# Layernorms, first scans and head queries begun before the stage or batch ahead has ended, in an eight-stage kernel

## What is computed

```
x = x + tanh(g) * mamba0(ctx, layernorm(x))        # 16 states, scan over 512 steps; z = layernorm(x)
x = x + tanh(g) * ffn0(layernorm(x))               # silu(x Wg) * (x Wu), 2 of 4 kept, Wd
x = x + tanh(g) * attention1(layernorm(x), ctx)
x = x + tanh(g) * ffn1(layernorm(x))               # ternary weights, 1408 wide
x = x + tanh(g) * mamba2(ctx, layernorm(x))
x = x + tanh(g) * ffn8(layernorm(x))               # weights rounded to float8
x = x + tanh(g) * attention3(layernorm(x), ctx)    # 16 heads of 128, rms-normed q and k
x = x + tanh(g) * bitnet(layernorm(x))               # needs mean |w| of both weights
# mamba, for each batch and state n, over the steps t:
h[t] = h[t-1] * exp(delta[t] * A[n]) + delta[t] * u[t] * B[n, t];   y[t] += h[t] * C[n, t]
```

## Time and profile before

| | us |
|---|---|
| median of three runs | 4097.34 (4094.35 to 4101.24) |
| profiled execution | 4101.41 |
| its span | 4099.8 |
| PE busy in it | 3705.4 |

### The profile page before, as it was taken

How to read it: one execution, slowest core, us unless ns; L and a number is a source line. 1 busy time by engine, 2 the same in 40 slices (tenths; PEclk the granted TensorE clock), 3 DMA queues, 4 the chain that set the end, 5 groups by cost and what they waited for, 6 DMA issues and landing times.

```text
span 4099.8 us, 41151 instructions
## 1 busy us (share of the span) xinstructions
PE 3705.4 (90%) x12733; PEld 1930.0 (47%) x12786; DVE 2992.1 (73%) x4855; ACT 1751.3 (43%) x2729; POOL 666.2 (16%) x647
## 2 busy tenths in 40 slices
PE   5989898889999998899995899899999999999787
PEld 3565555644444444444442444455455455454343
DVE  6777777759889797889889655467377377377398
ACT  4767676742323222333441111055255255254276
POOL 1433343433324210233320000000000000000000
PEclk8999999999999999999997999999999999999899
DMA  3323222342332422443333000022012021022000
GB/s 106 111 96 110 97 103 99 127 169 88 144 148 79 156 75 69 162 176 130 142 141 149 1 1 0 27 83 73 28 55 73 19 72 55 28 72 73 0 11 31
DMA packets 92134, 346.28 MB, mean 84 GB/s; under 512 B 12161, under 2 KB 20481, under 8 KB 78497
## 3 DMA queue, kind: packets, MB, share of 16 engines
q1 hardware_dynamic: 61888, 226.90, 15.5%
q0 software_dynamic: 30048, 116.94, 8.3%
HBM read 281.40 MB, written 62.39 MB: 84 GB/s over the span
## 4 chain that ended last, share of the span: by engine, by line
PE 58%; DVE 23%; issue 10%; ACT 6%; DMA 3%; POOL 0%; DVEq 0%; ACTq 0%; SPq 0%; POOLq 0%
PE ps L1009 38%; PE ps L1354 5%; PE ps L1083 4%; PE ps L1344 3%; PE ps L1231 2%; PE ps L1179 2%; DVE room L1504 2%; DVE room L1508 2%; PE ps L1076 2%; DVE room L1512 1%; DVE stat L1466 1%; DVE room L1517 1%; DMA room<-bc_scratch 1%; ACT room L729 1%; DVE ln L1482 1%
## 5 line engine op out<-in xcount | busy, mean ns | idle before, releaser
L1009 PE MATMUL ps<-lnT,room 128*128 128x512 f32 x2240 | 989.8, 598 | 26.0 <-DVE room L1698 10.2
L1009 PE MATMUL ps<-room 128*128 128x512 bf16 (+1 forms) x2873 | 936.6, 483 | 64.9 <-DVE xres L1970 19.6
L587 POOL TENSOR_TENSOR idle<-idle 128x1 f32<-128x1 f32 x288 | 474.7, 1648 | 1501.8 <-ACT room L792 554.9
L1009 PEld LDWEIGHTS ps<-lnT,room 128*128 128x128 f32 x2240 | 426.7, 191 | 573.3 <-issue 534.0
L1009 PEld LDWEIGHTS ps<-room 128*128 128x128 bf16 (+1 forms) x2912 | 398.1, 139 | 581.8 <-issue 324.1
L1179 PE MATMUL ps<-room 128*128 128x512 f32 x864 | 378.7, 596 | 8.4 <-DVE room L1650 8.4
L666 ACT ACTIVATE room<-room,small 128x511 f32<-128x511 f32 x256 | 163.6, 709 | 365.7 <-DVE room L1508 351.4
L1009 PE MATMUL ps<-down_rows,room 128*128 128x256 f32 x1024 | 250.1, 400 | 47.6 <-ACT room L786 46.9
L1565 DVE TENSOR_TENSOR_SCAN room<-room 128x2048 f32<-128x2048 f32 x64 | 283.1, 4424 | 6.2
L1508 DVE TENSOR_TENSOR_SCAN room<-room 128x2048 f32<-128x2048 f32 x64 | 283.4, 4428 | 5.4
L1934 DVE TENSOR_REDUCE stat<-ps 128x1 f32<-128x512 f32 x256 | 177.0, 692 | 132.0 <-PE ps L1009 132.0
(11 more groups left out here) (216 smaller groups left out, 4907.3 us busy)
## 6 DMA issues: line engine op xcount, KB each, us to landing
kv_stash<-room POOLq DMA_DIRECT2D x128, 256.0 KB, 2.8
room<-in_ffn SPq DMA_DIRECT2D x16, 2048.0 KB, 10.8
room<-bc_scratch POOLq DMA_DIRECT2D x128, 256.0 KB, 3.6
room<-kv_stash SPq DMA_DIRECT2D x64, 512.0 KB, 3.5
room<-stash POOLq DMA_DIRECT2D x24, 1024.0 KB, 9.5
room<-in_ffn SPq DMA_DIRECT2D x20, 1024.0 KB, 5.0
room<-in_ffn SPq DMA_DIRECT2D x12, 1536.0 KB, 7.8
room<-bc_scratch SPq DMA_DIRECT2D x64, 256.0 KB, 3.7
```

Of the source, the lines that this page charges most:

```text
L587: nc.gpsimd.tensor_tensor(idle[:, :], idle[:, :], idle[:, :], ALU.add).then_inc(zeros_added, 1)
L1009: last = nc.tensor.matmul(out, lhsT, rhs, start=(i == 0), stop=(i == len(parts) - 1))
```

## The change

**Mamba0.** The layernorm of batch b moves from the end of batch b - 1 to state 9 of batch b. Multiply and scan of state 0 of batch b + 1 (now `state_of`) go from that batch's beginning to the end of batch b, ahead of the products with z; SP loads its row of B at the end of batch b, and DVE waits for the store of B and C ahead of state 14. In the last batch ffn0's first layernorm stands there instead, and PE and ACT begin ffn0 without waiting for x.

```diff
+sp.wait_ge(bc_stored[0], 16)
+sp.dma_start(m_bc[0], bc_row(0, 0, 0)).then_inc(bc_loaded[0], 16)
 def body(b, last):
     for n in range(DS):
-        row = bc_row(0, b, n)
-        if n == 0:
-            sp.wait_ge(bc_stored[0], b * 16 + 16)
-        sp.wait_ge(scan_done, b * DS + max(n - (NBC - 1), 0))
-        sp.dma_start(m_bc[n % NBC], row).then_inc(bc_loaded[n % NBC], 16)
-        if n == 0:
+        if n:
+            row = bc_row(0, b, n)
+            sp.wait_ge(scan_done, b * DS + (n - 1))
+            sp.dma_start(m_bc[n % NBC], row).then_inc(bc_loaded[n % NBC], 16)
+        if n == 1:
...
+    if not last:
+        row = bc_row(0, b + 1, 0)
+        sp.wait_ge(scan_done, b * DS + (DS - 1))
+        sp.dma_start(m_bc[0], row).then_inc(bc_loaded[0], 16)
 batches(sp, body)
...
-if s == 1:
-    if not isinstance(b, int):
-        sp.wait_ge(b_wabs, b)
-    sp.dma_start(f_bit, bit_d[:, bass.ds(b * BIT_CHUNK, BIT_CHUNK)]).then_inc(b_abs_loaded, 16)
...
+    sp.wait_ge(w_rounded, TILES[2] - EARLY)
+    for c in range(B):
+        if c:
+            sp.wait_ge(b_wabs, c)
+        sp.dma_start(e_bit, bit_d[:, c * BIT_CHUNK:(c + 1) * BIT_CHUNK]).then_inc(b_abs_loaded, 16)
 def attention1(stage):
...
-sp.wait_ge(x_done, B * stage)
+sp.wait_ge(b_wabs, B)
 batches(sp, body)
```

GpSimd (POOL), which feeds the second mamba's states:

```diff
+pool.dma_start(s_delta, stashed(0, 0)).then_inc(s_delta_loaded, 16)
+pool.dma_start(s_du, stashed(1, 0)).then_inc(s_du_loaded, 16)
 def body(b, last):
-    before = b * WAITS + (s * B * WAITS + B * KV_WAITS)
-    wait(s_dA_ready, state(s, b, 0), before)
-    pool.dma_start(s_delta, stashed(0, b)).then_inc(s_delta_loaded, 16)
-    wait(s_dBu_ready, state(s, b, 0), before + 1)
-    pool.dma_start(s_du, stashed(1, b)).then_inc(s_du_loaded, 16)
-    wait(s_y_stored, b * 16 + s * B * 16, before + 2)
+    before = b * WAITS + (s * (B * WAITS - 2) + B * KV_WAITS)
+    wait(s_y_stored, b * 16 + s * B * 16, before)
     for j in range(STATES):
-        wait(s_dBu_ready, state(s, b, j), before + (3 + 2 * j))
+        wait(s_dBu_ready, state(s, b, j), before + (1 + 2 * j))
-        wait(s_hC_ready, state(s, b, j), before + (4 + 2 * j))
+        wait(s_hC_ready, state(s, b, j), before + (2 + 2 * j))
-    wait(s_y_added, state(s, b, STATES), before + (WAITS - 1))
+    at = before + (1 + 2 * STATES)
+    if not last:
+        wait(s_dA_ready, state(s, b, STATES), at)
+        pool.dma_start(s_delta, stashed(0, b + 1)).then_inc(s_delta_loaded, 16)
+        wait(s_dBu_ready, state(s, b, STATES), at + 1)
+        pool.dma_start(s_du, stashed(1, b + 1)).then_inc(s_du_loaded, 16)
+    wait(s_y_added, state(s, b, STATES), at + (0 if last else 2))
 batches(pool, body)
```

ScalarE (ACT), ffn, ffn8 and attention3:

```diff
 def ffn(stage, s):
-    act.wait_ge(x_done, B * stage)
+    if s:
+        act.wait_ge(x_done, B * stage)
     def body(b, last):
-        state_decay(s, b, 0)
         for t in range(T):
...
-    for j in range(1, STATES):
-        if scan_tile(T, j - 1) + 1 == t:
+    for j in range(STATES):
+        if (scan_tile(T, j - 1) + 1 if j else 0) == t:
 if not last:
...
+    act.wait_ge(e_split, b + 1)
     if not last:
-        act.wait_ge(e_split, b + 1)
+    else:
+        take_lnT(stage + 1, 0)
 batches(act, body)
...
 def start(b):
-    act.wait_ge(h_qp, b * H)
-    take_lnT(stage, b)
+    if not (isinstance(b, int) and b == 0):
+        act.wait_ge(h_qp, b * H)
+        take_lnT(stage, b)
```

TensorE (PE), ffn, ffn8 and attention3:

```diff
 def ffn(stage, s):
-    pe.wait_ge(x_done, B * stage)
+    if s:
+        pe.wait_ge(x_done, B * stage)
...
-for t in range(NT):
+for t in ((3, 0, 1, 2) if last and g == 3 else range(NT)):
     for j in range(n):
...
+pe.wait_ge(sg_ready, (b + 1) * T + base)
+pe.wait_ge(h_ready, (b + 1) * T + base)
 if not last:
-    pe.wait_ge(sg_ready, (b + 1) * T + base)
-    pe.wait_ge(h_ready, (b + 1) * T + base)
+else:
+    transpose_ln(stage + 1, 0)
...
-def start(b):
-    transpose_ln(stage, b)
-    pe.wait_ge(lnT_ready, b + (B * LNT[stage] + 1))
-    queries(b, 0)
-    queries(b, 1)
 def project(b, t):
-    product(ps[:, 4 + t, :], [(h_out3[:, h, t * P:(t + 1) * P], wo3[:, h, :]) for h in range(H)]
+    product(ps[:, PROJ[t], :], [(h_out3[:, h, t * P:(t + 1) * P], wo3[:, h, :]) for h in range(H)]
...
 if not last:
-    start(b + 1)
+    transpose_ln(stage, b + 1)
+if not last:
+    pe.wait_ge(lnT_ready, b + (B * LNT[stage] + 2))
+    queries(b + 1, 0)
 if not last:
+    queries(b + 1, 1)
...
+pe.wait_ge(lnT_ready, B * LNT[stage] + 1)
+pe.wait_ge(e_bank3, 1)
+queries(0, 0)
-pe.wait_ge(b_sum, 2)
-start(0)
+queries(0, 1)
+pe.wait_ge(b_sum, 2)
 batches(pe, body)
```

VectorE (DVE), mamba, ffn, ffn8 and attention3:

```diff
-elif not (isinstance(b, int) and b == 0):
-    dve.wait_ge(tile_filled, batch_tiles(b - 1, False)("z", NT - 1)[0] + 1)
 for t in range(NT):
...
+def state_of(b, n):
+    Bn = m_bc[n % NBC].unsqueeze(1).broadcast_to([P, NE, S])
+    h = m_h[n % 2]
+    dve.wait_ge(bc_loaded[n % NBC], b * (DS // NBC * 16) + (n // NBC + 1) * 16)
+    link(v.tensor_tensor(t3(h, NE), t3(m_du, NE), Bn, ALU.mult))
+    dve.wait_ge(dA_ready, b * DS + (n + 1))
+    v.tensor_tensor_scan(h, m_dA[n % 2], h, 0.0, ALU.mult, ALU.add).then_inc(scan_done, 1)
 def body(b, last):
-    for n in range(DS):
-        Bn = m_bc[n % NBC].unsqueeze(1).broadcast_to([P, NE, S])
-        h = m_h[n % 2]
-        dve.wait_ge(bc_loaded[n % NBC], b * (DS // NBC * 16) + (n // NBC + 1) * 16)
+    for n in range(1, DS):
-        link(v.tensor_tensor(t3(h, NE), t3(m_du, NE), Bn, ALU.mult))
-        dve.wait_ge(dA_ready, b * DS + (n + 1))
-        v.tensor_tensor_scan(h, m_dA[n % 2], h, 0.0, ALU.mult, ALU.add).then_inc(scan_done, 1)
+        if n == 14 and not last:
+            dve.wait_ge(bc_stored[0], b * 16 + 32)
+        state_of(b, n)
...
+if n == 9:
+    layernorm(stage, b)
...
-    layernorm(stage, b + 1)
+    dve.wait_ge(tile_filled, tile("h", DS - 2, NT - 1)[0] + 1)
+    state_of(b + 1, 0)
+else:
+    dve.wait_ge(tile_filled, tile("z", NT - 1)[0] + 1)
+    layernorm(stage + 1, 0)
...
-    dve.wait_ge(x_loaded, 16 * B)
-    layernorm(stage, 0)
+    state_of(0, 0)
+    dve.wait_ge(x_loaded, 16 * B)
-    n = DS + front + 1
-    chain.batches_peeled(n + front + 1 + LN_LINKS, n, body)
+    n = DS + front + 1 + LN_LINKS
+    chain.batches_peeled(n + front + 1, n - 1 + LN_LINKS, body)
 def gate_mamba(stage):
...
-layernorm(stage, 0)
+if s:
+    layernorm(stage, 0)
 def body(b, last):
...
-    if s == 1 and g == 2:
-        dve.wait_ge(b_abs_loaded, b * 16 + 16)
-        v.tensor_reduce(stat[:, bass.ds(b + 120, 1)], f_bit, AX.X, ALU.add, apply_absolute_value=True
-                        ).then_inc(b_wabs, 1)
 if last and s == 0:
...
+def sum_abs(c):
+    dve.wait_ge(b_abs_loaded, c * 16 + 16)
+    v.tensor_reduce(stat[:, bass.ds(c + 120, 1)], e_bit, AX.X, ALU.add, apply_absolute_value=True
+                    ).then_inc(b_wabs, 1)
 def body(b, first, last):
...
+    if g == 0 and not first:
+        sum_abs(b - 1)
+    if g == 2 and last:
+        sum_abs(B - 1)
+    if g == 1 and last:
+        layernorm(stage + 1, 0)
 if not last:
-for t in range(NT):
-    dve.wait_ge(ffn_done, (b + B * 2) * NT + (t + 1))
+for i, t in enumerate((3, 0, 1, 2) if last else range(NT)):
+    dve.wait_ge(ffn_done, (b + B * 2) * NT + (i + 1))
-    if t < NT - 1:
+    if last and t == 3:
+        ins.then_inc(e_bank3, 1)
+        dve.wait_ge(e_bank3, 1)
+    elif i < NT - 1:
...
+    def add(t):
+        dve.wait_ge(h_proj, b * NT + (t + 1))
+        return add_x(stage, b, t, ps[:, PROJ[t], :])
     if not last:
-        take_sums(b + 1, 0)
-        normalize(b + 1, 0)
-    for t in range(NT):
-        dve.wait_ge(h_proj, b * NT + (t + 1))
-        ins = add_x(stage, b, t, ps[:, 4 + t, :])
-    ins.then_inc(x_done, 1)
+    add(0)
+    add(1)
+    if not last:
+        take_sums(b + 1, 0)
+        normalize(b + 1, 0)
+    add(2)
+    add(3).then_inc(x_done, 1)
-layernorm(stage, 0)
```

22 lines of the change are left out of this document (12 added, 10 removed).

## The result

The changed kernel takes 4040.6 us in the median of four runs (4036.4 to 4046.5), beside 4099.3 (4094.4 to 4102.7) for the kernel before: ratio 0.9859, 95% interval 0.9842 to 0.9876, so 59 us less by the medians, 51 to 65 by the interval. The forecast was 4013 in a range of 3993 to 4050: the direction and the range held, the size was 84.5 where it became 59. The profiled execution is the fastest of the four: 4036.4, its span 4034.7, 65.1 less than the span before.

What follows compares the result with a forecast made beforehand. PE, busy 90% of the span, bounds the kernel, so gains come from its idle and half-clock time. 18 + 10.5 + 35 + 0 + 14 + 7 = 84.5 us off gives 4013 against the median, range 3993 to 4050.

Steps and rivals of the forecast that it cites:

- C: ffn1: the reduction, its 2 MB load and the decay waiting for delta go; 35 us gained, 22 to 39.
- F: Three joints of attention3: query products between projections hide ACT's copies; 7 us gained, 5 to 9.
- E: ffn8 to attention3: transposes stand before down(3), scores run sooner and at full clock; 14 us gained, 12 to 16.
- A: Mamba's three batch joints: state 0 scanned before the joint, layernorm hidden, ACT late next; 18 us gained, 15 to 22.
- The first rival: Mamba joints: ACT's branch doesn't limit them, so they give 36 us instead of 18; 3995 us, chance 0.10.
- B: Mamba to ffn0: layernorm hidden, PE begins 12 us sooner, DVE's first state step 9.3; 10.5 us gained, 8 to 14.
- less 4 for gaps that stay in the middle batches: ffn1: 4 us taken off the gain, as y is still stored and read back ahead of B.
- the second rival: ffn1: waits only shift, y stored, read back and then B keeps DVE late; 17 us gained, 4031 us, chance 0.18.
- D: ffn8: the four reductions, 4.39 us each, now stand here on an idle DVE; 0 us, 10 lost if PE waits.
- The slower rivals: Early loads of delta and du share the DMA with the weights and DVE waits for B; 4150 us, chance 0.02.

Runs made afterwards that it cites:

- actflat: The changed kernel with ACT's mamba loop written out four times, no branch back at the three joints: 4030.7 us, ratio to before 0.9829.
- noB: The changed kernel with ffn0's first layernorm back behind x, and PE and ACT waiting for x: 4048.8 us, ratio to before 0.9874.
- bfirst: The changed kernel with the next batch's first rows of B and C loaded ahead of the store of y: 4018.5 us, ratio to before 0.9795.
- sumback: The changed kernel with the four sums of \|w\| and their 2 MB loads back in ffn1: 4051.0 us, ratio to before 0.9874.

## Why the prediction was right where it was, and where not

**Bound and method** held in the main: the gain is PE's idle time, its work is the same. The half clock that was counted as gain (7.5 in C, 2.1 in F, some 3.5 in E) did not come in sum: PE's busy time is 3705.4 and 3702.6 in the two traces of before, 3702.5 and 3706.7 in the two of the changed kernel. What the joints gave back of it was lost again elsewhere.

**A.** Right at the joints: 18 forecast, and the three joints together became 17.5 us shorter (57.0 to 39.5), with ACT named as what is late next. `actflat` shows that ACT's branch is that: 5.10 us of ACT with the branch, none in straight code. By the Trainium skill ("Runtime: NRT & Kernel Launch", Instruction fetch mechanics) a taken branch to code outside the prefetched window stalls until that code is fetched. The traces agree that there is a stall; that a fetch is its cause no run shows. The first rival, that the branch doesn't limit, is refuted. The step that failed is one the prediction never wrote down: it summed the joints as if the batches between them stayed as they were. The insides of the second and third batch together became 3 to 5 us longer (373 to between 376 and 378, in every trace), of which 3.4 are the two more long products; the last batch varies between 166 and 174. PE's gap behind ACT's copy, at the first two joints, was 7.5 and 8.0 where 6 to 7 was said. The joints' shares were 2.6, 4.3 and 10.5 for 4.5, 4.5 and 9, the third 8 to 9 in traces where the product behind the gap is long. The layernorm at state 9 of the last batch, priced at up to 7.5, is not to be told from none: the last batch takes 171.4 in the mean of the eleven traces that have it, 170.3 in that of the two without.

**B.** Right in both steps: PE's 12.2 us, and DVE's first state step 10.3 sooner, where 9.3 was said (its own terms, 870.26 and 9, give 879.3 and 9.5); by `noB` the part is worth 8 to 10.

**C.** The causes were right, the size was not. The term that failed is the "less 4 for gaps that stay in the middle batches": it measured 12.2 in PE's gaps, plus about 4 of half clock behind them. It left out how late the row of B is. In the trace before, the row landed 16 us after y, hidden behind the late Silu; after the change it landed 17 us after y, and nothing hid it. With delta and du out of its way it landed 5.1 us after its issue instead of 9.0, but the store of y, behind which it waits, took 9.7 instead of 5.2: by the sorting of the stores about 2 of these 4.5 by the weight load that now stands ahead of the store, and 2 more by the early loads beside both. That is the mechanism of the second rival, y stored and then B, at 11 of its 18 us: 24 of 35 us remained, not 17. `bfirst` settles that the row is what is waited for: with it out of that order, ffn1 is 529 to 531 us, 41 less than in the profiled execution before and 6 more than I counted. The sums were the largest piece (14 us by `sumback`); the other two edits do the same thing, and together bring 4 at most, within the spread of two traces.

**D.** Right: nothing in ffn8 moved.

**E.** Right in the sum (13.4), wrong in one piece: the scores take 5.20 us and not 3.7 (5.2 to 6.6 in all traces), behind the wait for the keys, which stayed; and the square of the second head is not quite hidden (1.15).

**F.** Right at the joints, and by luck in the sum. From the idle time ahead of the layernorm's transposes to the first transposed keys the three joints take 171 us in the three traces with the old order and 160.5 to 165.7, in the mean 163.3, in the eleven with the new one: 7.6 gained. But from the first scores to the end it is 1411.1 to 1414.6 with the old order and 1406.8 to 1415.3 with the new one, in the mean 2 less. The other 5 were lost between the joints and in bitnet, as in A; why is open. The profiled execution after is the shortest of the eleven: two of its layernorm gaps (2.0, 1.7, 1.8 before) fell to 0.4, which no other trace repeats.

**The slower rivals** did not come. The early loads do collide, but with the store of y and the weights, not with the rows of B along the batch.

## What to carry to other kernels

Follow a queue to its end: what counts is when the last thing that the waiting engine needs was issued, and a transfer that stands ahead of it can grow when an edit elsewhere brings it beside other loads. A wait that another one hides is not small, it only does not show yet. When two edits serve the same wait, undo them one by one and together, since each alone looks worthless. And when a joint gets shorter, measure the stretches between the joints as well, in more than one pair of traces: here a part of 2 us looked like one of 7.8.

## What the runs showed of the hardware

ACT loses 4.6 to 5.1 us at the taken loop branch of mamba (four joints in the two profiled executions), and nothing where the same code is written out. A sum product behind the same wait of 2.4 us takes 3.72 or 5.41 us, and the kernels with shorter gaps at the joints have more of the long ones between them (5 instead of 3 in the second and third batch, in each of twelve traces). Why is open. A 1 MB store from on-chip memory takes 4.5 to 5.4 us where a weight load of 768 KB is issued up to 3 us behind it, and 7.1 to 10.8 where that load is issued up to 0.7 us ahead, the longer the more other loads run beside them.
